# The QKV projection of a 128-token window, made in one step of an attention loop or in three

## The reference, cut to what matters

```python
def local_attention(q, k, v):          # 8 heads of 64; windows of 128 tokens
    ...                                # each window sees itself and the one before it
    sim = jnp.einsum('bhwid,bhwjd->bhwij', bq, bk)
    sim = jnp.where(mask, -max, sim)
    attn = jax.nn.softmax(sim, axis=-1)
    return jnp.einsum('bhwij,bhwjd->bhwid', attn, bv)

def _layer(x, wqkv, qs, ksc, wo, lg, lb, w1, b1, w2, b2):
    qkv = shift_token(x) @ wqkv        # 256 features -> 3 x 512
    q, k, v = jnp.split(qkv, 3, axis=-1)
    q = l2norm(q) * qs
    k = l2norm(k) * ksc
    q, k = rotary_xpos(q, k)
    x = x + local_attention(q, k, v) @ wo
    ...                                # layer norm, up projection, gelu gate, down projection
for l in range(2):
    x = _layer(x, ...)
```

## Time and profile before

| | us |
|---|---|
| median of 3 runs | 2154.39 (2153.69 to 2154.58) |
| the profiled execution, its own time | 2154.2 |
| its span, first to last instruction | 2152.4 |
| PE busy | 1969.0 (91%) |
| DVE busy | 1466.1 (68%) |
| ACT busy | 1261.3 (59%) |
| POOL busy | 757.0 (35%) |

### The profile page before, as it was taken

One profiled execution on the slowest core, in us unless ns is written; L12 is line 12 of the kernel. 1 busy time (PEld: TensorE's weight loads), 2 busy tenths in 40 slices (PEclk: granted clock), 3 DMA queues, 4 the chain that ended last, 5 costly groups with the idle time before them and its releaser, 6 DMA issues.

```text
span 2152.4 us, 36235 instructions
## 1 busy us (share of the span) xinstructions
PE 1969.0 (91%) x12064; PEld 1246.0 (58%) x12064; DVE 1466.1 (68%) x3928; ACT 1261.3 (59%) x3013; POOL 757.0 (35%) x632
## 2 busy tenths in 40 slices
PE   7978999999897669999999999998999999999998
PEld 4522333333234447777677676676777677777766
DVE  7778888888862557568567567557757756856854
ACT  4526666666664337647547646645755764754763
POOL 1033221121322466056146136336515605604610
PEclk9969999999999879999999999999999999999999
DMA  6667534535315620000000000023001000000000
GB/s 181 165 116 149 67 47 61 68 51 97 64 66 146 183 84 1 21 20 1 21 15 6 21 11 11 1 81 113 2 20 40 2 20 30 11 21 20 21 1 30
DMA packets 105447, 112.28 MB, mean 52 GB/s; under 512 B 49801, under 2 KB 84273, under 8 KB 104241
## 3 DMA queue, kind: packets, MB, share of 16 engines
q1 hardware_dynamic: 104688, 101.06, 20.8%
q0 software_dynamic: 576, 8.91, 1.1%
HBM read 67.21 MB, written 42.47 MB: 51 GB/s over the span
## 4 chain that ended last, share of the span: by engine, by line
PE 47%; DVE 6%; ACT 6%; issue 3%; POOL 3%; DVEq 0%; ACTq 0%; POOLq 0%
PE qkv_ps L1370 11%; PE s_ps L1416 5%; PE pt_ps L1487 5%; PE s_ps L1474 4%; PE o_ps L1512 3%; PE qkv_ps L1432 3%; PE pt_ps L1559 3%; POOL inv_norm L1840 2%; PE o_ps L1474 2%; PE pt_ps L1474 2%; PE s_ps L1432 2%; ACT x_all L1685 2%; PE o_ps L1559 2%; PE turn_ps L1396 2%; PE turn_ps L1496 1%
## 5 line engine op out<-in xcount | busy, mean ns | idle before, releaser
L690 ACT ACTIVATE probs<-st_ps 128x512 f32<-128x512 f32 (+3 forms) x768 | 330.0, 495 | 165.5 <-PE st_ps L595 164.9
L1370 PE MATMUL qkv_ps<-w_qkv,x_parts 128*128 128x512 f32 x1152 | 312.6, 416 | 26.6 <-DVE x_all L1932 18.8
L580 PE MATMUL s_ps<-k_stack,q_stack 96*128 96x512 bf16 (+3 forms) x768 | 242.6, 347 | 36.5 <-DVE piece_negmax L735 25.6
L735 DVE CUSTOM_DVE_ANT_0 att_in<-s_ps,causal 128x128 f32<-128x128 f32 (+3 forms) x512 | 233.5, 484 | 42.1 <-PE s_ps L580 42.0
L1370 PEld LDWEIGHTS qkv_ps<-w_qkv,x_parts 128*128 128x128 f32 x1152 | 216.9, 197 | 76.6 <-issue 33.6
L1955 DVE CUSTOM_DVE_ANT_0 x_all<-s_ps,band 128x256 f32<-128x256 f32 (+1 forms) x512 | 178.4, 402 | 112.0 <-PE s_ps L1416 111.3
L1685 ACT ACTIVATE x_all<-x_all,negmax 128x256 f32<-128x256 f32 (+1 forms) x512 | 249.4, 491 | 6.3 <-DVE negmax L1955 5.4
L595 PE MATMUL st_ps<-q_stack,k_stack 98*128 98x512 bf16 (+3 forms) x768 | 241.3, 335 | 12.3 <-ACT probs L690 10.1
L1707 ACT COPY att_in<-pt_ps 128x512 f32<-128x512 f32 (+1 forms) x256 | 143.0, 559 | 149.0 <-PE pt_ps L1487 147.6
L817 POOL TENSOR_SCALAR_AFFINE_SELECT probs<-probs 128x512 f32<-128x512 f32 x128 | 81.4, 636 | 414.6 <-ACT probs L690 414.6
L1848 POOL TENSOR_TENSOR x_all<-x_all,turn_by 128x512 f32<-128x512 f32 x128 | 180.0, 1427 | 101.6 <-PE turn_ps L1396 56.9
(11 more groups left out here) (150 smaller groups left out, 3406.6 us busy)
## 6 DMA issues: line engine op xcount, KB each, us to landing
qk_scratch<-parts SPq DMA_DIRECT2D x64, 192.0 KB, 2.8
q_stack<-qk_scratch SPq DMA_DIRECT2D x96, 128.0 KB, 6.7
k_stack<-qk_scratch SPq DMA_DIRECT2D x96, 128.0 KB, 7.1
w_ffn<-ffn_weights POOLq DMA_DIRECT2D x4, 2176.0 KB, 11.5
x_in<-xt_scratch SPq DMA_DIRECT2D x16, 512.0 KB, 4.2
ffn_weights<-w_high SPq DMA_DIRECT2D x2, 2176.0 KB, 7.7
ffn_weights<-w_raw SPq DMA_DIRECT2D x2, 2176.0 KB, 13.4
att_scratch<-att SPq DMA_DIRECT2D x32, 128.0 KB, 2.0
```

The costliest lines, as they stand in the source:

```text
L580: pe.matmul(s_ps[i % 3][:, 0:kw], q_stack[0:STK, slot, h, qt * P:(qt + 1) * P], k_stack[0:STK, slot, h, k0:k0 + kw], start=True, stop=True ...
L690: act.activation(probs[:, n % 3, h, q0:CH], st_ps[i % 3][:, q0:CH], ACT.Exp).then_inc(exp_done.sem, 1)
L735: dve.tensor_tensor_reduce(seen[:, i % 3, 0:kw], s_ps[i % 3][:, 0:kw], causal[:, CH - kw:CH], -1.0, BIG, ALU.add, ALU.min, result).then_in ...
L1370: mm = pe.matmul(qkv_ps[:, part * CH:(part + 1) * CH], x_parts[:, w % XR, xp, k, :], w_qkv[:, wp, k, part * INNER:(part + 1) * INNER], sta ...
```

## The change

PE makes all three parts of a window in step p = 1 of its loop, and none in steps 2 and 3. Nothing on any other engine is changed, and no instruction is added or removed.

```diff
                     if u == 2:
                         project(it, AHEAD, 2)
-                    if p >= 1 and 0 < w < NT - AHEAD:
-                        project(it, w + AHEAD, p - 1)
+                    if p == 1 and 0 < w < NT - AHEAD:
+                        for part in range(3):
+                            project(it, w + AHEAD, part)
                     if OUT_AT <= u < OUT_AT + KD:
                         project_out(it, 0, u - OUT_AT)
```

## The result

The changed kernel takes 2235.97 us (median of 4 runs, 2234.39 to 2237.98), the kernel before 2154.04 in the same comparison (4 runs). The ratio is 1.0374, 95% interval 1.0361 to 1.0386: 3.7% slower, as forecast (2233). The profiled execution has a span of 2233.3 us against 2152.4, 80.9 us more.

What follows compares the result with a forecast made beforehand. PE's work and a closed circle over PE, ACT, DVE and POOL were both taken as full. 2154.2 + 70.6 (circles) + 8 (clock) = 2232.8, given as 2233 us, 3.7% slower; range 2205 to 2257.

Steps and rivals of the forecast that it cites:

- The bound: In the loop's windows, PE's work and a circle through square, sums, POOL's power and unit vectors each fill 12.41 us.
- The scores behind the burst: Second scores of a window start 4.20 us after its projection starts, not 1.57; window period goes from 12.4 to 14.60.
- Both routes to the sums agree: Before the sums, masks and low_x free DVE at 8.48 us and square allows them at 8.51.
- PE's idle time of 2.3 us in three places: Per window, PE waits 0.8 us for copied probabilities, 0.8 for the copy of q, 0.7 for unit vectors.
- Four circles in each of 8 iterations, nothing given back: First projection to output projection grows from 49.58 to 58.40 us, 8.82 per iteration, 70.6 in all, none recovered later.
- The clock: PE's short idles around the transposes of k lower its clock in some circles: 0 to 16 us, 8 taken.
- nothing was absorbed: Rival: DVE and ACT catch up on late scores; half absorbed 2190 us, chance 8%; all absorbed 2154 us, 2%.
- the circle did not get shorter: Rival: square follows the earlier part 1 at once, circle 10.3 us, PE alone bounds, 2138 us; chance 3%.
- the clock did not fall in most circles: Rival: the clock falls in 24 to 32 circles at 1.5 us each, 2261 to 2273 us; chance 12%.

Runs made afterwards that it cites:

- the experiment: Changed kernel with square one step earlier on ACT, ahead of the copy and exponentials it stood behind: 2190.34 us, ratio 1.0155 to the kernel before.
- the other execution of the same kernel: The changed kernel run once more, unedited, to look at its clock: 2228.33 us in one execution.
- the aside: Kernel before, with the sums of window 3 put ahead of low_x on DVE in window 0: 2146.54 us, ratio 0.9945.

## Why the prediction was right, step by step

- *The bound* (PE and a closed circle, both full): right. Reordering has shortened the four circles together in none of the kernels; the only gain came from ahead of them, in window 0.
- *The scores behind the burst*: right. Expected after the burst's start and measured: scores 4.20 and 4.36, mask 5.63 and 5.79, exponentials 6.45 and 6.60, square 7.45 and 7.60, sums 8.51 and 8.64, unit vectors 13.23 and 13.35, next burst 14.60 and 14.72. The only miss is the first term: 18 matmuls ahead of scores take 4.36 us, not the 4.20 that I read where other 512-column matmuls follow them. Everything behind carries these 0.16 along, less 0.04.
- *Both routes to the sums agree*: wrong, without effect. `low_x` took 0.42 us, not 1.53, so DVE was free a microsecond before square was done. With square out of the way the circle fell by 1.1 us, as the experiment shows.
- *PE's idle time of 2.3 us in three places*: 2.0 us by the releasers in the window shown. The wait for the copied probabilities was 0.51 (0.8 expected), for q 0.34 (0.8) and for the unit vectors 0.97 (0.7), with 0.17 for `scale_output`, which I had not named. I put too much on ACT, here as in three of the expectations.
- *Four circles in each of 8 iterations, nothing given back*: right. 8 x 9.28 = 74.2 us, where 70.6 were forecast.
- *The clock*: near in size by luck, wrong in place. I took 8 us, for falls in the 32 new circles. But for the first of an iteration there was none in either profile of the changed kernel: those circles are all 14.71 to 14.76 us. What came is three more falls in window 1, behind a wait that is as long as before, and a longer one in iteration 4. Summed over the first stretch of all iterations, the comparison's profile has 79.8 us more than before, of which 74.2 are circles, so some 5.5 us are the clock. In the other execution of the same kernel the sum is 74.6 us more, so the clock added 0.4 us. The term is a matter of the execution, and this one happened to lie near the forecast. One burst of the comparison's profile that ran partly at the lower clock, with 1.41 us of idle ahead of it, and 1 us of it by windows (granted clock 0.50, 1.2 GHz of 2.4):

```profile
1161.36 5.98 PE L1370 MATMUL qkv_ps<-w_qkv,x_parts 128*128 128x512 f32 x18 [1.41 <-DVE x_all L1933]
```

```profile
1162.00:1163.00 1.00, 1.00 (x4) 0.81 (x3) 1.00 (x1) 0.00 (x0) 1.00 (x2) 0.50 0.00 0
```

  The Trainium skill's warning on short idles between groups of matmuls ("TensorE: Matmul & The Clock Gate", "A second HAM failure mode: psum-queue depth-cycling") would have put the sum at the upper end. The trace does not bear it out for the new circles: their idles of 0.34 and 0.97 us drew no fall in either profile. Those of 0.76 and 1.41 us (0.88 in iterations 5 to 7; 1.9 and 2.1 in iteration 4, which the prediction did not set apart) ahead of the first burst do in some iterations, and so did 0.76 and 0.79 us in two iterations of the aside. What sets the two places apart is not shown.
- *The rivals*: nothing was absorbed, the circle did not get shorter, and the clock did not fall in most circles. The 80.9 us by which the profiled execution is longer are 74.2 + 5.5 + about 1 us outside the first stretches. The forecast had 70.6 + 8, so a circle term 3.6 us too small and a clock term 2.5 us too large partly cancel.

## What to carry to other kernels

Before moving filler work on the busiest engine, list what the first instruction behind it releases on each other engine, and what stands behind that in those queues: here six to twelve more matmuls ahead of a score group held back a squaring whose own input had come early. A closed circle over several engines can be as full as the busiest engine itself, and then delays in it count in full, once for each turn. Work it out from the starts of consecutive instructions in the right surroundings; a duration read beside other neighbours was the largest error in the circle.

## What the runs showed of the hardware that was not expected

`low_x` is one DVE instruction of 128 x 256 elements with both inputs in SBUF. It took 1.53 us in the kernel before and 0.42 in the changed one. What differs is what POOL does meanwhile. Before, POOL's addition was under way when `low_x` started at 1000.36, and `low_x` ended 0.29 us after it:

```profile
999.20 2.40 POOL L1853 TENSOR_TENSOR x_all<-x_all,rot_s 128x1024 f32<-128x1024 f32 x1 [0.42 <-DVE rot_s L1946]
```

After, POOL was idle from 1003.24 to the clamp of the next window, and `low_x` ran at 1004.39:

```profile
1000.88 2.36 POOL L1854 TENSOR_TENSOR x_all<-x_all,rot_s 128x1024 f32<-128x1024 f32 x1 [0.76 <-DVE rot_s L1947]
1007.27 0.25 POOL L1839 TENSOR_SCALAR sum_sq<-sum_sq 128x16 f32<-128x16 f32 x1 [4.03 <-DVE sum_sq L1927]
```

So the instruction ended shortly after the addition, as if it had been held until then. The Trainium skill ("SBUF — State Buffer", "Who interferes with whom") says that a DVE operation with two SBUF inputs and a GpSimd operation that reads SBUF take turns, the later one blocking until the first is done. The eleven traces agree with it for the addition: 212 of their `low_x` start while it is under way, and every one ends 0.28 to 0.38 us behind its end, whether that makes it 0.42 or 2.61 us long. The 367 that start with no POOL instruction under way take 0.40 to 0.43 us. They do not agree for the power (line 1841, 16 elements a partition, from SBUF too): the 125 that start during it take 0.41 to 0.42 us and end before it does. For this change it meant a microsecond of slack on DVE that the prediction did not see.
